# Graph attention in steps of 1024 edges, with one TensorE signal a step and a lead of four steps

## What is computed

```python
h  = relu(layernorm(x));  gl = h @ Wl.T;  gr = h @ Wr.T          # 4 heads x 16
score = (att * leaky_relu(gl[src] + gr[dst], 0.2)).sum(-1)       # per edge and head
m     = segment_max(score, src);  ex = exp(score - m[src])
alpha = ex / (segment_sum(ex, src)[src] + 1e-16)
out   = segment_sum(gr[dst] * alpha, src)
x     = x + gelu(concat([out, h]) @ W1.T + b1) @ W2.T + b2
```

## Time and profile before

| | us |
|---|---|
| median of 3 runs | 9896.93 |
| their range | 9879.18 to 9920.47 |
| span of the profiled execution | 10034.3 |
| first to last start of attention's gathers | 1151.5 to 7277.3 |
| busy: PE, DVE, POOL, ACT | 3861.6, 4726.8, 4978.3, 752.2 |

### The profile page before, as it was taken

One profiled execution on the slowest core, in us unless ns is written; L12 is line 12 of the kernel. 1 busy time (PEld: TensorE's weight loads), 2 busy tenths in 40 slices (PEclk: granted clock), 3 DMA queues, 4 the chain that ended last, 5 costly groups with the idle time before them and its releaser, 6 DMA issues. The chain is left out here.

```text
span 10034.3 us, 108018 instructions
## 1 busy us (share of the span) xinstructions
PE 3861.6 (38%) x25399; PEld 3480.9 (35%) x25400; DVE 4726.8 (47%) x10656; ACT 752.2 (7%) x1207; POOL 4978.3 (50%) x4913
## 2 busy tenths in 40 slices
PE   1011123444444444444444444444484333333445
PEld 1011112434343434333343434343472233333443
DVE  8999634454545454545544454445462122222222
ACT  3011101000000000000000000000000000000000
POOL 0000265555454545555565545454504666666664
PEclk9965555555555555555555555555555555555555
DMA  2000011212121212122121212121611111111111
GB/s 20 0 0 0 19 41 41 57 49 59 49 57 49 57 49 58 48 54 54 48 59 50 58 48 58 48 58 48 56 53 40 43 45 44 44 44 42 44 44 33
DMA packets 498404, 444.25 MB, mean 44 GB/s; under 512 B 178490, under 2 KB 394682, under 8 KB 498018
## 3 DMA queue, kind: packets, MB, share of 16 engines
q0 software_dynamic: 156672, 160.75, 9.9%
q1 hardware_dynamic: 340050, 279.02, 9.3%
q10 hardware_dynamic: 1296, 0.22, 0.0%
HBM read 325.70 MB, written 113.85 MB: 44 GB/s over the span
## 5 line engine op out<-in xcount | busy, mean ns | idle before, releaser
L815 POOL DMA_INDIRECT rows<-gr_table,stage x3328 | 3357.3, 1009 | 3730.8 <-DVE stage L998 2756.7
L1329 POOL DMA_INDIRECT message<-h_table,edge_stage x1568 | 1605.4, 1024 | 854.2 <-issue 464.0
L868 PE MATMUL bank<-gl_parts,hot_t 128*128 x10008 | 772.3, 241 | 2781.7 <-ACT hot_t L951 1738.1
L868 PEld LDWEIGHTS bank<-gl_parts,hot_t 128*128 128x128 bf16 x10008 | 680.3, 131 | 2912.2 <-issue 2887.3
L854 PE MATMUL bank<-terms,hot_sum 128*128 128x68 f32 x6656 | 1588.6, 422 | 6.6 <-DVE terms L1027 6.4
L854 PEld LDWEIGHTS bank<-terms,hot_sum 128*128 128x128 f32 x6656 | 1516.2, 333 | 8.7 <-DVE terms L1027 6.3
L1356 PE MATMUL bank<-message,edge_hot 128*128 128x64 f32 x3136 | 720.5, 424 | 1490.0 <-DVE message L1401 1338.8
L1356 PEld LDWEIGHTS bank<-message,edge_hot 128*128 128x128 f32 x3136 | 683.7, 330 | 1526.9 <-DVE message L1401 1371.0
L1011 DVE TENSOR_TENSOR z<-bank,rows 128x256 f32<-128x256 f32 x832 | 349.9, 421 | 1408.3 <-remote 1283.2
L1050 DVE TENSOR_TENSOR acc<-acc,bank 128x68 f32 x832 | 187.2, 225 | 1712.3 <-remote 1529.8
L951 ACT COPY hot_t<-bank 128x512 bf16<-128x512 bf16 x834 | 488.0, 585 | 5311.7 <-remote 4099.8
(11 more groups left out here) (266 smaller groups left out, 3405.4 us busy)
## 6 DMA issues: line engine op xcount, KB each, us to landing
gr_rows<-rows SPq DMA_DIRECT2D x832, 128.0 KB
rows_again<-gr_rows SPq DMA_DIRECT2D x832, 128.0 KB
rows<-gr_table,stage POOLq DMA_INDIRECT x3328
edge<-in_edge_attr SPq DMA_DIRECT2D x195, 256.0 KB
message<-h_table,edge_stage POOLq DMA_INDIRECT x1568
gr_table<-gr SPq DMA_DIRECT2D x1, 1536.0 KB
h_table<-h_sb SPq DMA_DIRECT2D x1, 1536.0 KB
out<-x_sb SPq DMA_DIRECT2D x1, 1536.0 KB
```

The source lines that it names most:

```text
L815: pool.indirect_dma_start(rows[k][:, g, :], None, m.gr_table[:, :], bass.IndirectOffsetOnAxis(stage[k][:, g:g + 1], 0)).then_inc(s_gath[k] ...
L868: last = pe.matmul(bank[2 + slot][:, g * D:(g + 1) * D], hot_t[slot][:, g * P:(g + 1) * P], m.gl_parts[:, bass.ds(blk, 1), part * D:(part ...
L1329: pool.indirect_dma_start(rows[k][:, e, :], None, m.h2_table[:, :], bass.IndirectOffsetOnAxis(stage[k][:, e:e + 1], 0)).then_inc(s_gath[k] ...
```

## The change

A step has now 8 tiles (1024 edges, two groups); a chunk has 32 steps, the kernel 416.

- `decode` writes each edge's place within its block and each penalty to HBM tables, in sorted order (`place_rows`, `pen_rows`).
- SP loads a step's 1024 places onto all 128 partitions (`place_b`, 4 buffers, 256 KB a load). DVE compares them with the partition's number in one bf16 operation, which gives `hot_t` directly. PE's transposes, ACT's copies and the comparison on the other side are gone.
- PE's left products run 4 steps ahead of DVE (`LAG`), in 4 PSUM banks, and the sums are taken by DVE 4 steps after their terms, from 4 more banks. After a step's left products and sums PE gives one increment, `s_step`. DVE awaits it at the start of its step and takes both results with it.
- POOL has 8 slots of 8 gathers instead of 16 of 4.
- `scan` runs forward and backward over the scores themselves, takes the row ends of both directions in one round trip through PE, and takes the maximum of both results. Penalties come by 4 DMAs from ACT's queue. The small scans of the four heads are one. The correction for a straddling node touches its block alone.

Core of the diff (waits and operations that the text speaks of):

```diff
-            def hot_of(out, q):
-                at = m.place[:, bass.ds(q * GROUP_TILES, GROUP_TILES)].unsqueeze(2).to_broadcast([P, GROUP_TILES, P])
-                return dve.tensor_tensor(out[:, :, :], places, at, ALU.is_equal)
+            def hot_of(q, slot, place_slot, loads):
+                dve.wait_ge(s_place[place_slot], loads)
+                dve.tensor_scalar(hot_t[slot][:, :], place_b[place_slot][:, :], m.iota_node[:, 0:1], None, ALU.is_equal
+                                  ).then_inc(s_hot, 1)
...
+            def load_place(q, slot):
+                at_least(sp, s_hot, q - V + 1)
+                sp.dma_start(place_b[slot][:, :], m.place_rows[bass.ds(q, 1), :].to_broadcast([P, STEP])
+                             ).then_inc(s_place[slot], 16)
...
                     if part.score:
-                        sp.wait_ge(s_gath[k], (j + 1) * 16 * GROUP_TILES)
-                        sp.dma_start(m.gr_rows[bass.ds(score_group(j, k), 1), :, :].rearrange("q p f -> p (q f)"),
+                        load_place(q + LAG + 2, (k + LAG + 2) % V)
+                        sp.wait_ge(s_gath[k], (j + 1) * 16 * STEP_TILES)
+                        sp.dma_start(m.gr_rows[bass.ds(q, 1), :, :].rearrange("q p f -> p (q f)"),
...
+            def body(part, j, first):
+                for k in range(U):
+                    q = U * j + k
+                    if part.score:
+                        last = left(q + LAG, k % LAG)
+                    if part.sum:
+                        last = scatter(q - CHUNK_STEPS, k % LAG)
+                    last.then_inc(s_step, 1)
...
+                    dve.wait_ge(s_step, q + 1)
+                    if part.score:
+                        dve.wait_ge(s_gath[k], (j + 1) * 16 * STEP_TILES)
+                        dve.tensor_tensor(z[:, :, :], bank[k % LAG][:, 0:SW].rearrange("p (g f) -> p g f", f=D),
+                                          rows[k][:, :, :], ALU.add).then_inc(s_z, 1)
+                        hot_of(q + LAG, k % LAG, (k + LAG) % V, place_loads(j, k + LAG))
...
+                        at_least(dve, s_gath[(k - 1) % U], (j + (k > 0)) * 16 * STEP_TILES)
+                        stage_of((k - 1) % U, q + U - 1).then_inc(s_staged, 1)
...
+                chain.link(dve.tensor_tensor_scan(fore[:, :], pen_s[:, 0:SCAN], score_s[:, :], -BIG, ALU.add, ALU.max))
+                chain.link(dve.tensor_tensor_scan(top[:, down], pen_s[:, 1:SCAN + 1][:, down], score_s[:, down], -BIG,
+                                                  ALU.add, ALU.max))
```

More of the change, by code:

```diff
@@ L703, in attention @@
     V = 4
[L704 to L715, removed]
-    terms = [sb(f"terms{k}", [P, PAIRS, ACCW], F32, ctx) for k in range(2)]
+    outer = CHUNK_STEPS // U
+    SW = STEP_TILES * D
+    PAIRS = STEP_TILES * HEADS
+    rows = [sb(f"rows{k}", [P, STEP_TILES, D], F32, ctx) for k in range(U)]
+    rows2 = [sb(f"rows_again{k}", [P, STEP_TILES, D], F32, ctx) for k in range(V)]
+    stage = [sb(f"stage{k}", [P, STEP_TILES], I32, ctx) for k in range(U)]
+    place_b = [sb(f"place_b{k}", [P, STEP], BF16, ctx) for k in range(V)]
+    hot_t = [sb(f"hot_t{k}", [P, STEP], BF16, ctx) for k in range(LAG)]
+    hot2 = [sb(f"hot_sum{k}", [P, STEP_TILES, P], F32, ctx) for k in range(LAG)]
+    z = sb("z", [P, STEP_TILES, D], F32, ctx)
+    leaky = sb("leaky", [P, STEP_TILES, D], F32, ctx)
+    weighed = sb("weighed", [P, STEP_TILES, D], F32, ctx)
+    terms = [sb(f"terms{k}", [P, PAIRS, ACCW], F32, ctx) for k in range(LAG)]
     scores = sb("scores", [P, CHUNK_TILES, HEADS], F32, ctx)
@@ L781, in __init__ @@
             self.sum = not known or c >= 1
-            self.turned = 0 if known and c == 0 else turned_before(c)
     def loop(eng, part, body):
-        body(part, part.c * steps, True)
-        with eng.Fori(part.c * steps + 1, part.c * steps + steps) as j:
+        body(part, part.c * outer, True)
+        with eng.Fori(part.c * outer + 1, part.c * outer + outer) as j:
             body(part, j, False)
@@ L933, in _ @@
-            for q in range(2):
-                turn_hot(q, q)
-                left(q, q)
+                    pe.wait_ge(s_inits, c + 1)
+                    pe.matmul(bank[7][:, 2:3 + HEADS], m.ones[0:1, :], again[:, :], start=True, stop=True)
+                else:
+                    pe.wait_ge(s_inits, c + 1)
+                for v in range(2):
+                    last = pe.transpose(bank[7][:, v:v + 1], inits[0:1, v, :], m.ident[0:1, 0:1])
+                last.then_inc(s_inits_ps, 1)
@@ L937, in turn @@
+                pe.wait_ge(s_exp, c + 1)
+                for g in range(ROW_TILES):
+                    last = pe.transpose(bank[6 + g // HALF][:, g % HALF * P:(g % HALF + 1) * P],
+                                        score_s[:, g * P:(g + 1) * P], m.ident[:, :])
+                last.then_inc(s_back_ps, 1)
+            for q in range(LAG):
+                left(q, q).then_inc(s_step, 1)
             def turn(part):
@@ L1004, in body @@
-                    tile = (U * j + k) * GROUP_TILES - part.c * CHUNK_TILES
+                    q, r = U * j + k, U * j + k - CHUNK_STEPS
+                    add = part.sum and not (first and k < LAG)
+                    tile = q * STEP_TILES - part.c * CHUNK_TILES
                     if not isinstance(tile, int):
-                        tile = nc.s_assert_within(tile, 0, CHUNK_TILES - GROUP_TILES, skip_runtime_bounds_check_because=
-                                                  "a step's groups are its chunk's")
+                        tile = nc.s_assert_within(tile, 0, CHUNK_TILES - STEP_TILES, skip_runtime_bounds_check_because=
+                                                  "a chunk's steps are its tiles")
```

472 lines of the change are left out of this document (208 added, 264 removed).

## The result

The changed kernel takes 9491.58 us (median of 4 runs, 9474.44 to 9516.23); the kernel before took 9901.39 on the same chip (9879.18 to 9920.47). The ratio is 0.9578, 95% interval 0.9548 to 0.9608. So it is 4.2% faster where 14.6% was forecast, and the time lies 240 us above the upper end of the range.

A forecast was written before the change was run, and what follows sets the result against it. The prediction took waits among POOL, DVE and PE as the bound, then POOL's gathers. POOL's stretch 4430 + 195 + 50 = 4675 against 6126 (-1450), ends -20: 8564 us profiled, times 0.9863 is 8450 us; range 8200 to 9250.

The forecast's parts named there:

- Signals and lead: Attention loop: PE sends one signal per 8 tiles instead of 6, needed four steps later, a cover of about 33 us.
- the term of 50 us for held signals: Attention loop: 50 us added for held PE signals that outlast the cover, bounds 0 to 700.
- What bounds the kernel: Attention: a ring of waits, POOL for DVE's stage lists and DVE for PE's signals, held back while POOL issues gathers.
- POOL's stretch, 4675: Attention's gathers: 4430 us of steps, 195 for scans and 50 for held signals, against 6126 before, so -1450.
- The step's 10.65: Attention: POOL's 8 gathers set a step of 10.65 us, within 10.3 to 10.7; 416 steps make 4430 us.
- DVE, 5.9 us a step: Attention: DVE's work per step of 8 tiles sums to 5.9 us, at most 6.7, wholly hidden under POOL.
- Rival D: Attention: place loads arrive late, a step takes 18.05 us, the kernel some 11500 us; chance 0.04 together with C.
- C: Attention: DVE locks POOL out, every gather takes 2.27 us, the kernel 11290 us; chance 0.04 together with rival D.
- The scan, 28 us: Scans between chunks: about 28 us each, plus 35 for holds, mostly under POOL's staged 74 us; 195 us in all.
- Ends, -20: Outside POOL's attention stretch: shorter DVE tail after the last gather and decode changes, together -20 us, within 20 either way.
- Rival A: Attention: every PE signal is held until POOL stops, 12.3 us a step, all scans open, 9245 us; chance 0.22.
- B: Attention: nothing is lost, POOL at 1.25 us a gather throughout, all scans hidden, 7940 us; chance 0.06.

The follow-up runs named there:

- e7: Changed kernel with one of three bf16 parts in the left products, 24 matmuls a step instead of 40, on chip 0: 9145.38 us, ratio 0.9243 to the kernel before.
- e6: The kernel before, unaltered, profiled on chip 0 (first kind): 9879.86 us, ratio 0.9994.
- f14: The kernel before, unchanged, traced on chip 7 (second kind): 8160.4 us.
- e5: The changed kernel, unaltered, on chip 0 (first kind): 9473.11 us, ratio 0.9571 to the kernel before.
- e9: Changed kernel with 14 more PE increments a step that nobody waits for, on the second kind of chip: 8217.07 us, ratio 1.0074 to the kernel before.
- e1: Changed kernel with one of three parts in the left products, 24 matmuls a step instead of 40, on chip 11 (second kind): 8224.78 us, ratio 1.0084.

## Why the prediction was wrong

**The step that failed** is "Signals and lead", and with it the term of 50 us for held signals (0 to 700). The prediction read the earlier trace rows as one signal held until POOL stops, and the earlier trace rows as proof that single signals get through; so fewer of them, needed later, had to help. It was right that the result comes late and not the matmul's start. What the runs showed in place of its price is that the delay goes with PE's work and not with the number of signals: with the same signals and 16 of 40 matmuls less, e7 gains 328 us. The delay grows with what is queued in front (up to 53 us, where the longest hold that was known was 21.7), and the number of matmuls fell only from 48 to 40 for 8 tiles, while the signals fell from 6 to 1. A lead of four steps covers a delay of 33 us, but no rate. The working "5.8 us of PE in a step of 10.65" took PE's busy time at the pace of a pause and made it a cover; in the burst shown above the same 40 matmuls took 16.6 us.

The size can be worked out from pairs of the same kernel on the two kinds, as us more for 8 gathers divided by the matmuls that go with them:

| | first kind | second kind | more | matmuls | ns each |
|---|---|---|---|---|---|
| before, attention | 14.48 (e6) | 10.81 (f14) | 3.67 | 48 | 76 |
| after, attention | 13.48 (e5) | 10.94 (e9) | 2.54 | 40 | 64 |
| one left part | 12.76 (e7) | 10.95 (e1) | 1.81 | 24 | 75 |
| message loop, before | 11.79 (e6) | 10.76 (f14) | 1.03 | 16 | 64 |
| message loop, after | 11.85 (e5) | 10.87 (e1) | 0.98 | 16 | 61 |

(The message loop's figures are from the first to the last start of its gathers, over 196 groups. e9 stands for the changed kernel, with its added signals.) 61 to 76 ns a matmul over a threefold range of their number is near a proportion, but not one: between 40 and 24 matmuls of the same kernel the difference, 0.73 us, is 46 ns for each of the 16. It is an estimate over the whole stretch, not a price of one matmul; and since matmuls, columns and busy time went together in all of these, it doesn't tell which of them counts.

Point by point:

- **What bounds the kernel**: right that it was the ring POOL, DVE, PE; wrong about what its weak link costs, and true of one kind of chip only.
- **POOL's stretch, 4675**: measured 5645 on the result's chip, 970 more. From z to z: within chunks (403 steps, the first chunk's 31 at 13.18 and the rest at 11.88) 4828 us against 403 x 10.65 = 4292, 536 more; at the 12 changes of chunk 70.3 us each, 843, against 12 x 10.65 and the 195, 520 more. (Less the 50 for holds, the one interval that this count has not, and the 27 us by which z's stretch is longer than the gathers', these are the 970, but for rounding.) On the second kind the stretch is 4550 to 4556, below the forecast: there the scans, 41 us from z to z, cost POOL nothing, and the step is 10.94 instead of 10.65.
- **The step's 10.65**: its 0.44 us for a collision was the right size; it is met twice a step (0.41 and 0.49), where 10.65 has room for one and a half: 10.0 + 0.90. Here the prediction set a rule of the Trainium skill aside too soon. The Trainium skill ("SBUF — State Buffer", Who interferes with whom) has a DVE instruction with two SBUF inputs contend with a GpSimd instruction that reads SBUF, and not one with at most one SBUF input outside the 2-port modes. The traces agree for leaky, terms, z and the reduction. Whether the comparisons against a scalar, which hold a gather too, run in a 2-port mode no run here shows. The gather at 5045.99 that spoke against it began 0.14 us before hot_sum and lost nothing; the one at 5052.53 began 0.13 after hot and lost the rest of it. The page gives the pair to whichever starts first for its whole instruction. The gathers agree: one that starts second loses what is left of DVE's operation, less 0.12 us, and one that starts first loses nothing. So a step costs 0.9 us more and not the 4.0 that the prediction had worked out for it by adding DVE's operations in full. In the other direction they differ: by the page DVE would be blocked behind a gather that started first, but in e1 the 370 hot_sum comparisons that began during a gather took 1.21 us at the median, and the 45 that began beside none 1.22.
- **DVE, 5.9 us a step**: 2345.9 us in e9's stretch of 416 steps, scans included, are 5.6. The bf16 comparison, taken at 0.4 between 0.19 and 1.21, costs 0.49.
- **SP's queue**: nothing, as said; DVE waited 0.5 us for places in all. Rival D is out, and C too: the median gather is 944 ns.
- **The scan, 28 us**: 28.7 (4260.0 to 4288.7). But in front of it stand 34 us in which PE works off the last four steps' sums and the next steps' left products between them: in the window above 32 matmuls in 20.5 us beside the gathers, then, with POOL's staged steps used up, 77 in 14.5 us. The prediction had these as "the last step's 12", and so 63 + 12 us against 74 of cover; POOL pauses some 49 us per scan.
- **Ends, -20**: -71. The rest of the span is 3837.9 us and was 3908.5; 50 of it lie between the last gather of attention and the first of the message loop (333 and 283 us).
- **Rival A**, 9245, came nearest, though it held single signals until POOL stops and not a backlog of matmuls: bursts and pauses, "remote" in front of z, and 5645 / 84 = 67 us a cycle where it had 55.4. Its loop of 12.3 us a step was near the 11.88 measured; it was short of the result by the drains at the changes of chunk. B is the second kind of chip in its mechanism (scans hidden), with stretched gathers left over. That the result fell on a chip where either could be seen was not in the prediction's hands: no row told that chips differ.
- **The sum against the median**: the profile of before was 1.4% over its median, that of after 0.1% under (9483.1). Taking the 1.4% over to the new kernel made the forecast 114 us too low, and the 8 us of the new profile come on top.

970 - 51 + 114 + 8 = 1041 us, which is what lies between 8450 and 9491.

**What stays open.** What slows PE's results on the first kind: that it comes from POOL's gathers is shown only by its coming and going with them in the trace, since no run without them fell on such a chip. Whether it goes by matmul, column or busy time (the signals that somebody waits for are ruled out by e7 as the whole of it, added ones were not tested there); and what property of a chip makes it. A kernel that pauses POOL for each step's gathers, and one with two of three left parts, were not tried.

## What to carry to other kernels

A lead or a deeper buffer covers a delay, not a rate: before a wait is moved off the path, check in the trace that the engine waited for can do its whole work per step beside the others, by counting its instructions in windows of undisturbed overlap and by how long after a matmul's start its signal is acted on, and not by its busy time or by its starts alone. Where an engine's results come late, take away work of that engine first (16 of 40 matmuls: 328 us; twice the lead: nothing). And time a change on several chips: here the same kernel takes 17 to 18% less on one kind than on the other, and the change is a gain of 4.2% on one and a loss of 0.7% on the other.

## What was unexpected of the hardware

- The same kernel takes 9885 to 9901 us in two sets of runs (the result's and chip 0) and 8142 to 8193 on six chips, at the same granted clock and the same 944 to 947 ns a gather. Only the loops with matmuls beside GpSimd's indirect gathers differ. On the first kind PE's results come up to 53 us after a matmul's start, and the starts are 0.7, 1.4 or 2.1 us apart once some 30 matmuls are unreported (14 matmuls in 20 us, 5 in 14); on the second a step's 16 sums take 3.68 us without a gap in full gather traffic.
- On the first kind PE is back at full pace only some us after the last gather's end: 3.7 us in the stretch shown (4041.36 to 4045.06), 3.2 at the median of 76 pauses of POOL.
- A gather that begins during a DVE operation with two SBUF inputs is longer by what is left of it, less 0.12 us: 0.41 and 0.49 us beside leaky and terms, up to 1.07 in the changed kernel. If the gather begins first, it loses nothing. A direct copy of GpSimd of the same size is issued in 534 ns instead of 944.
